# State-space block between two mixture-of-experts layers: the running sums reach all partitions through memory instead of through TensorE

## The reference

```python
dt = softplus(dt_raw + dt_bias)
log_a = A * dt
cum_log_a = jnp.cumsum(log_a, axis=2)
log_diff = cum_log_a[:, :, :, None, :] - cum_log_a[:, :, None, :, :]
L = jnp.exp(jnp.where(causal, log_diff, -jnp.inf))
CB = jnp.einsum('bcign,bcjgn->bcijg', C_c, B_c)
y_intra = jnp.einsum('bcijGH,bcijG,bcjGH,bcjGHp->bciGHp', L_rs, CB, dt_rs, x_rs)
...
y_inter = jnp.einsum('bciGH,bciGn,bcGHnp->bciGHp', decay_from_start, C_c, state_at_start)
```

## Time and profile before

| | |
|---|---|
| median of 3 runs | 2400.81 us |
| profiled execution, device time | 2399.49 us |
| its span | 2397.7 us |
| PE busy | 2338.3 us, 98% |
| DVE, ACT, POOL busy | 59%, 40%, 28% |
| granted TensorE clock, mean | 0.995 |
| chain that ended last, by engine | PE 95%, DVE 2%, issue 1%, ACT 1%, DMA 1% |

### The profile page before, as it was taken

One profiled execution on the slowest core, in us unless ns is written; L12 is line 12 of the kernel. 1 busy time (PEld: TensorE's weight loads), 2 busy tenths in 40 slices (PEclk: granted clock), 3 DMA queues, 4 the chain that ended last, 5 costly groups with the idle time before them and its releaser, 6 DMA issues.

```text
span 2397.7 us, 41942 instructions
## 1 busy us (share of the span) xinstructions
PE 2338.3 (98%) x16732; PEld 2061.0 (86%) x16732; DVE 1413.8 (59%) x3236; ACT 955.8 (40%) x1665; POOL 665.3 (28%) x524
## 2 busy tenths in 40 slices
PE   5999999999998999999999999998999999999998
PEld 5999999777798888888888888887999999877787
DVE  6777762223228777777777777777777764232221
ACT  4332322333336455544545555454333332233321
POOL 1244443121221322222222222221044444121221
PEclk9999999999999999999999999999999999999999
DMA  7644213899844111111111111103254320799958
GB/s 254 197 156 150 85 63 125 265 279 281 242 99 130 36 28 27 27 27 27 27 27 27 27 27 27 27 18 135 84 195 145 109 97 20 255 286 276 282 117 176
DMA packets 102754, 292.82 MB, mean 122 GB/s; under 512 B 22498, under 2 KB 22754, under 8 KB 91872
## 3 DMA queue, kind: packets, MB, share of 16 engines
q1 hardware_dynamic: 55216, 198.87, 23.2%
q0 software_dynamic: 47344, 91.27, 17.0%
HBM read 197.28 MB, written 151.80 MB: 146 GB/s over the span
## 4 chain that ended last, share of the span: by engine, by line
PE 95%; DVE 2%; issue 1%; ACT 1%; DMA 1%; DVEq 0%; SPq 0%; ACTq 0%
PE m_p_ab L1569 5%; PE m_p_ab L1571 5%; PE m_p_ab L1570 5%; PE m_p_x L1569 3%; PE m_p_x L1571 3%; PE m_p_x L1570 3%; PE p_up_a L697 3%; PE p_up_b L697 3%; PE p_gate_a L697 3%; PE p_up_a L699 3%; PE p_up_a L698 3%; PE m_p_y L1670 3%; PE p_gate_a L698 3%; PE p_gate_b L697 3%; PE p_gate_a L699 3%; PE p_x_b L797 3%
## 5 line engine op out<-in xcount | busy, mean ns | idle before, releaser
L1862 DVE SCALAR_TENSOR_TENSOR m_xt<-m_ssm,m_convw,m_xt 128x256 f32<-128x256 f32 x384 | 218.9, 583 | 57.5 <-ACT m_ssm L1438 48.4
L1569 PE MATMUL m_p_ab<-m_ht_hi,m_wi_b_hi 128*128 128x256 f32 x640 | 182.0, 284 | 3.9 <-ACT m_ssm L1438 2.3
L1571 PE MATMUL m_p_ab<-m_ht_hi,m_wi_b_lo 128*128 128x256 f32 x640 | 179.3, 280 | 0.0
L1570 PE MATMUL m_p_ab<-m_ht_lo,m_wi_b_hi 128*128 128x256 f32 x640 | 179.2, 280 | 0.0
L448 POOL DMA_INDIRECT slot_rows<-a_hr,a_slot_now x128 | 130.4, 1019 | 151.4 <-PE p_gate_a L699 96.2
L448 POOL DMA_INDIRECT slot_rows<-b_hr,b_slot_now x128 | 129.9, 1015 | 151.4 <-PE p_gate_b L699 96.1
L697 PE MATMUL p_gate_a<-a_hts_hi,a_w_hi 128*128 128x256 f32 x512 | 148.6, 290 | 1.7 <-DVE a_hts_lo L978 1.4
L697 PE MATMUL p_gate_b<-b_hts_hi,b_w_hi 128*128 128x256 f32 x512 | 148.4, 290 | 0.3
L697 PE MATMUL p_up_b<-b_hts_hi,b_w_hi 128*128 128x256 f32 x512 | 147.7, 289 | 0.0
L697 PE MATMUL p_up_a<-a_hts_hi,a_w_hi 128*128 128x256 f32 x512 | 147.7, 288 | 0.0
L699 PE MATMUL p_gate_a<-a_hts_hi,a_w_lo 128*128 128x256 f32 x512 | 145.4, 284 | 0.0
(11 more groups left out here) (352 smaller groups left out, 7440.5 us busy)
## 6 DMA issues: line engine op xcount, KB each, us to landing
a_ew<-in_ew SPq DMA_DIRECT2D x32, 1536.0 KB, 7.5
b_ew<-in_ew SPq DMA_DIRECT2D x32, 1536.0 KB, 8.3
after_ffn<-a_zeros POOLq DMA_DIRECT2D x6, 2048.0 KB
out<-b_zeros POOLq DMA_DIRECT2D x6, 2048.0 KB
slot_rows<-a_zeros POOLq DMA_DIRECT2D x1, 8336.0 KB, 36.9
a_rows<-slot_rows SPq DMA_DIRECT2D x32, 260.5 KB, 8.3
b_rows<-slot_rows SPq DMA_DIRECT2D x32, 260.5 KB, 9.0
a_xr<-in_x SPq DMA_DIRECT2D x8, 1024.0 KB
```

The source lines that it names most:

```text
L1569: t.matmul(out, l_hi, r_hi_, start=first, stop=False)
L1570: t.matmul(out, l_hi, r_lo_, start=False, stop=False)
L1571: return t.matmul(out, l_lo, r_hi_, start=False, stop=last)
L1862: ins_ = v.scalar_tensor_tensor(xt[:, m, :], ssm[:, m, i:i + BM], convw[:, m, i:i + 1], xt[:, m, :], ALU.mult, ALU.add)
```

## The change

All of it at once:

1. The constants are built inside the main program, ahead of POOL's other work; the other engines begin without them and wait for them where they are used.
2. Feed-forward: the first rows are loaded and normed in two halves, block 0 is normed from these rows and not from a second copy, its second turn has a PSUM tile of its own (`p_gate`), and fewer loads stand ahead of the first weight pieces.
3. Time steps: the hi and lo weights of the 8 columns lie side by side in one stationary tile of 40 columns (`w_dt`), so the projection has 8 matmuls in place of 12; the two halves are added when they are turned, by a plain product with `picks` in place of a transpose.
4. B by C goes to `p_y`, right behind `cumulate`, and DVE masks it from PSUM; ACT's copy is gone. The fifth gate part goes to `p_y` too. `p_ab` has one user less.
5. The running sums: `spread` on PE, `cum_rows`, `pick`, `cum_lo` are gone. SP writes `cum_t` to memory and loads it back to all partitions, straight into `cdec`; DVE's `differences` read `cdec`, and ACT's `carried` then takes the exponential in place.
6. DVE adds to the state ahead of the gating of chunk 0.

```diff
...
                 if not prior:
-                    v.memset(chosen_before[:], 0.0)
-                    norm_stats(0)
+                    norm_first(0)
                     split(0)
-                    norm_apply(0)
                     turned_s(0, 0)
                     turned_s(0, 1)
-                    for o in range(1, 4):
-                        split(o)
+                    split(1)
+                    norm_first(1)
+                    dve.wait_ge(c.built, c.BUILT)
+                    norm_apply(0)
+                    split(2)
+                    split(3)
...
+            def spread(n):
+
+                sp.wait_ge(cum_t_ready, n + 1)
+                sp.dma_start(cum_sums, cum_t[:]).then_inc(cum_written, 16)
+                wait(sp, y_full, n * TM)
+                sp.wait_ge(cum_written, 16 * (n + 1))
+                sp.dma_start(cdec_both[:, :, :, :].rearrange("p h j t -> p (h j t)"),
+                             cum_sums.rearrange("(o h) t -> o (h t)", o=1).to_broadcast([P, NH * BM])).then_inc(cum_spread, 16)
...
                 sp.wait_ge(prior.added, prior.BEFORE_LAST_ADDED)
+                spread(0)
                 for n in range(NM):
                     u = n % XM
+                    if n + 1 < NM:
+                        spread(n + 1)
                     sp.wait_ge(out_ready, n * TM + TM)
...
                 def carried(j):
 
 
-                    wait_apart(c, a, (cr_full, n * TM + j + 1), (y_full, n * TM))
+                    act.wait_ge(diff_ready, (n * TM + j + 1) * NH)
                     bias = {"bias": c.cut[:, n:n + 1]} if j == 0 else {}
-                    a.activation(cdec[j][:], heads(p_cr), ACT.Exp, **bias).then_inc(cdec_exp, 1)
+                    a.activation(cdec[j], cdec[j], ACT.Exp, **bias).then_inc(cdec_exp, 1)
...
+            def project_dt(n):
+                if is_(n, 0):
+                    pe.wait_ge(w_lo_done, 1)
+                    pe.wait_ge(gap_set, 1)
+                out = ab(n, J_DT)[0:CR, 0:BM]
+                for k in range(KD):
+                    for part in (ht_hi, ht_lo):
+                        mm = t.matmul(out, w_dt[:, k, :], part[:, k, :], start=(k == 0 and part is ht_hi),
+                                      stop=(k == KD - 1 and part is ht_lo))
+                mm.then_inc(ab_full, 1)
...
                 cumulate(n)
+                b_by_c(n)
                 if not is_(n, 0):
                     out_product(n - 1, 1)
                 ssm_part(2)
-                b_by_c(n)
-                spread(n, 0)
                 for m in range(3, 6):
                     ssm_part(m)
-                spread(n, 1)
                 for m in range(6, CI):
                     ssm_part(m)
...
             def differences(n, j):
 
-                dve.wait_ge(cdec_exp, n * TM + j + 1)
-                dve.wait_ge(y_full, n * TM)
+                dve.wait_ge(cum_spread, 16 * (n + 1))
+                wait(dve, y_full, n * TM)
                 for hd in range(NH):
-                    v.tensor_scalar(decay[j][:, hd, :], heads(p_cr)[:, hd, :], cum[:, 0, j, hd:hd + 1], 0.0,
+                    v.tensor_scalar(decay[j][:, hd, :], cdec[j][:, hd, :], cum[:, 0, j, hd:hd + 1], 0.0,
                                     ALU.subtract, ALU.min).then_inc(diff_ready, 1)
...
                     if more:
+                        add_state(n, 0)
                         gated(n, 0)
-                        add_state(n, 0)
```

More of the change, by code:

```diff
@@ L134, in __exit__ @@
             self.nc.all_engine_barrier()
[L137 to L182, removed]
-                   allow_small_or_imprecise_dtypes=True).then_inc(built, 1)
-            pool.wait_ge(built, c.BUILT)
@@ L299, in ffn @@
                  hr[2][:, :, :].rearrange("p j d -> p (j d)")[:, 0:PIECE]]
+        turned_in = lambda b, half: p_gate if b == 0 and half == 1 else p_ts
+        norms = lambda at: at // TS + 1 if at < TR else at // TR + 2
         uses = lambda o: slot_of[:o + 1].count(slot_of[o])
@@ L410, in program @@
                         sp.wait_ge(hr_ready, (b + 1) * TR)
+                        if b == 0 and not prior:
+                            sp.wait_ge(hs_mid, TS)
                         sp.dma_start(xr[:], src_r[b + 1]).then_inc(xr_loaded, 16)
@@ L702, in turn_s @@
                 pe.wait_ge(hs_ready, (b + 1) * TS)
-                wait(pe, hts_ready, 2 * b + half)
+                if b > 0:
+                    pe.wait_ge(hts_ready, 2 * b + half)
                 for kk in range(2):
@@ L706, in turn_s @@
                     for j in range(TS):
[L707 removed]
+                        mm = t.matmul(turned_in(b, half)[:, kk, j * P:(j + 1) * P], hs[:, j, k * P:(k + 1) * P], c.ident[:],
                                       is_transpose=True, start=True, stop=True)
@@ L993, in finish @@
                 dve.wait_ge(down_done, (b + 1) * UN)
+                if b == 0 and not prior:
+                    dve.wait_ge(xs_loaded[0], 16)
                 if b == NS - 1:
@@ L1144, in mamba @@
     CLEARED = len([name for name in prior.sems if name not in OWN])
-    JOBS = 6 + 2 * CI
-    J_DT, J_C, J_B, J_TOK, J_CUM, J_CB = 0, 1, 2, 3, 6, 8
-    J_SSM = [4, 5, 7, 9, 10, 11, 12, 13]
-    J_GATE = list(range(14, 22))
+    JOBS = 5 + 2 * CI
+    J_DT, J_C, J_B, J_TOK, J_CUM = 0, 1, 2, 3, 6
+    J_SSM = [4, 5, 7, 8, 9, 10, 11, 12]
+    J_GATE = list(range(13, 21))
+    IN_X, IN_Y = [J_GATE[2], J_GATE[3]], [None, J_GATE[4]]
+    RING = [job for job in range(JOBS) if job not in IN_X + IN_Y]
     with ExitStack() as ctx:
@@ L1213, in wi @@
         def wi(first, n):
+            if first == DT0:
+                return w_dt[:, :, 0:NH], w_dt[:, :, LO_AT:CR]
             if first < SPLIT_COL:
-                return [part[:, :, first:first + n] for part in wi_a]
+                return [part[:, :, first - NH:first - NH + n] for part in wi_a]
             i, at = divmod(first - SPLIT_COL, 2 * P)
```

233 lines of the change are left out of this document (139 added, 94 removed).

## The result

The changed kernel takes 2504.3 us (median of 4, 2500.7 to 2510.5) beside 2400.2 us for the kernel before on the same chip: ratio 1.043, 95% interval 1.0403 to 1.0458. It is slower by 104 us. The forecast was 2526 (2460 to 2570), slower with 0.94: the sign, the mechanism and the place hold, and the size came out 22 us too large.

What follows compares the result with a forecast made beforehand. TensorE, busy 98% of the span, was taken as the bound. Start -3, block 0 +19 and 15 blocks at +7.3 gave +125.5 us on the profiled 2399.5, so 2526 us against the median, range 2460 to 2570.

Steps and rivals of the forecast that it cites:

- differences from SBUF: VectorE's eight differences, read from SBUF, start 0.20 us apart and take 1.6 us; bounds 0.13 and 0.27 apart.
- clock, per block: After TensorE's gaps the granted clock drops, so the gate parts run slower: +1.7 us a block.
- a block: Each state-space block behind block 0 grows by 7.3 us: 5.6 from gaps less removed work, 1.7 from the clock.
- start: Loads begin earlier, but VectorE's weight splits and norms limit the gain before the first product: -3 us, bounds 0 and -6.
- block 0: SyncE issues the first write of the sums late, at 769.5, and they land about 777.2: +19 us.
- second feed-forward part: Its changes, the halving of one load, cost nothing behind the last block's matmuls.
- removed 2.75 us: TensorE's net saving a block: spreads 2.29, time steps 0.47, state wait 0.23, less 0.24 for the plain matmul.
- The waits: ScalarE's carried waits for differences, delaying copies of ssm 3 and 6; TensorE gaps of 3.2 and 5.1 us a block.
- The transfer: Write 2.8 us and read 4.9 us of the sums are hidden, landing 1.9 us before they are needed.
- Faster: Rival: no gaps, 16 x 2.75 = 44 us less work and 3 us at the start, 2354 us; chance 0.04.
- rival of smaller gaps: GpSimd's product does not hold up the convolution and the clock stays up; 2475 us; chance 0.20.
- late sums: Rival: sums land after 9.0 us, differences start 2.2 us later a block, 33 us more, 2560 us; chance 0.18.

Runs made afterwards that it cites:

- run 5: Changed kernel with GpSimd's first product (C and the first decay factors) made to wait until both groups of differences are done; 2476.2 us, ratio 1.0318.
- run 4: Changed kernel with useless matmuls added in TensorE's waits, 24 between ssm 4 and ssm 5 and 36 before the first gate part; 2482.4 us, ratio 1.0337.
- run 3: Changed kernel with only the transfer undone, TensorE spreading the running sums again; 2376.0 us, ratio 0.9896, and a second time 2382.9 us, ratio 0.9901.
- run 1: Changed kernel with only ScalarE's list reordered, copies of ssm 3 to 5 ahead of carried(0), later copies ahead of carried(1); 2402.2 us, ratio 0.9985.
- run 2: Changed kernel with only VectorE's list reordered, both groups of differences ahead of convolution 2 in blocks 1 to 15; 2377.9 us, ratio 0.991.
- run 8: Run 2's kernel with block 0's write and read of the running sums issued ahead of the last two pieces of weights; 2364.4 us, ratio 0.9863.

## Why the prediction was right, and where its sizes were off

Term by term, forecast and measured:

| term | forecast | measured |
|---|---|---|
| differences from SBUF | 0.20 us apart, 8 in 1.6 | 1.65 for 8 |
| first wait | 3.2 us, to t = 5.9 | 3.17, to 6.0 |
| end of second wait | t = 15.3 | 15.3 |
| GpSimd's product on a convolution | 1.5 us | 1.50 (run 5) |
| clock, per block | 1.7 us | 1.5 in the mean (run 4), 1.6 (run 5) |
| time steps and state wait, per block | -0.46 us | -0.79 (run 3) |
| a block | +7.3 us | +6.5 |
| start | -3 us | -4.0 to -4.2 |
| block 0 | +19 us | +21.5 |
| second feed-forward part | 0 | -9.9 |

- **The removed 2.75 us** of TensorE's work can't be seen alone. Its part without the spread was 0.46 us a block (time steps and state wait); run 3 gained 0.79.
- **The waits.** The step held in every number, and runs 1 and 2 cut its chain at both ends and got the 100 us back. The two waits of a block together are 5.4 to 8.1 us, 6.7 in the mean.
- **The start.** The first gate matmul came at 14.83, earlier than the 17 I had put there, but the first product only at 27.39, 3.3 us ahead of before: VectorE's splits and norms limit it, as argued.
- **The differences.** I chose 0.20 us apart between bounds, against the formula of the Trainium skill ("VectorE: DVE Perf Modes", in its section on the fixed extra latency per instruction), which gives 127 ns by estimate. The profile has eight in 1.65 us, 0.20 apart and 0.28 long each, so the choice was right and the sum by that formula would have been too small in this term. The same section says below its table that the fixed part measures about 150 cycles and not 58; with that the estimate is 223 ns.
- **The size of a block.** The forecast was 63.9 us and the trace has 63.1; over 15 blocks that is 12 of the 22 us. 0.33 of the 0.8 us is the removed work, of which I had counted too little (0.46 against 0.79). The rest, 0.4 us, lies between the end of the second wait and the transposes: I had 8 x 1.42 = 11.4 us for the gate parts and 1.7 for the clock, and the 13 blocks take 12.6 in the mean. I took the 1.7 from one wait of 2.28 us and charged it to every block. Its size was near (1.6 by run 5), and its place was not quite regular: two of the 13 blocks have no low clock there, and two have it for longer (64.19 and 64.34 us). The gate parts themselves go faster than 11.4 in the blocks of runs 4 and 5 that take 11.0 at full clock.
- **The second feed-forward part** was the step that failed outright: "cost nothing behind the last block's matmuls". I had costed the load's halving and not looked at TensorE's waits there, which stand in the trace of before (4.12 and 4.90 us, quoted in run 3). 7.0 us of them are gone, and with the clock that no longer falls the part is 9.9 us shorter. With 1 us more gained at the start than forecast and 2.5 us more lost in block 0, the terms account for 20 of the 22 us.
- **Block 0.** The write went out at 765.2, not 769.5, since the start and the shorter head brought everything forward; but the read could be issued only 4.3 us later, not 2.8, beside the stores and two loads, and landed at 776.5, not 777.2. The stretch from the softplus table to the first store grew by 21.5 us: TensorE came out of a wait of 23 us at a low clock (0.61 over the next 3.7 us) and met a second one of 5.6.
- **The transfer** is hidden in blocks 1 to 15, as forecast: the read is issued 1.4 us behind the write instead of 2.8, and the median landing is 4.7 us behind its issue against the 4.9 of the earlier trace rows. In the changed kernel the sums land 1.9 to 3.8 us before VectorE reads them, where the forecast had 1.9. With the differences moved ahead (runs 2 and 8) under 0.7 us of that is left.
- **The rivals.** "Faster" came true once the order was mended (runs 2 and 8): 2364 to 2378 us against the 2354 that it gave. For the kernel as it stood it needed an error in my reading of the waits, and that reading had none. The rival of smaller gaps fell with the 1.50 us of run 5 and the clock's 1.5; the late sums didn't come, since the read landed after 4.7 us.

## What to carry to other kernels

When an operand moves from PSUM to SBUF and an engine's wait moves from one producer to another, the price is not in the operation but in what is queued behind the wait: write down both engines' lists, put times on them, and see which buffer ring passes the delay on. Here the place of three lines was worth 126 us, and the matmuls saved 44 at most (2.75 in each of 16 blocks). Of several waits on one chain, look at the last first (here it was worth 78 us by itself, the first 20), and look through a table of waits also for the stages that a change touches only in passing.

## What I had not expected of the hardware

- The same two waits in neighbouring blocks met different clocks: behind second waits of 2.26 and 3.37 us the granted clock was 0.57 in one block and 1.00 in the next. The short wait was short because the low clock had already stretched ssm 5 to 7 before it.
- The same 96 matmuls of the gate parts, at a granted clock of 1.00 and without a wait, took 11.00 us in some blocks of run 4 and 11.41 in others, and 11.30 in the kernel before. No trace shows why.
- The write of 8 KB to memory was complete at most 1.4 us behind its issue in the steady blocks but one (the next issue waits for it), and 3.3 to 4.3 us behind it in block 0, where loads and stores of 0.5 to 1 MB ran beside it.
- An idle engine's early start cost 28 us: GpSimd's product, 2.4 us long and needed by nobody soon, held a convolution on the chain for 1.5 us a block.
